# Another order of GpSimd's round in the attention stage of a two-layer mixture-of-experts kernel

## The reference

```python
x = x + L0_ffn(L0_cond(x, W1, b1, v, itok_B_0_2), wg, w1, w2, w3, sw1, sw2, sw3)
x = x + L1_ffn(L1_cond(x, itok_B_0_30, W, b), ln1.., Wqkv, Wproj, ln2.., Wgate, W1, b1, W2, b2)
```

```python
# end of layer 0: each token adds up the rows that its 4 experts left for it, weighed
y = zeros.at[buf_tok].add(out * buf_w)
# layer 1, per sequence b
h = layernorm(xc); q, k, v = h @ Wqkv; q, k = rope(q), rope(k)
x = xc + (softmax(mask(q @ k.T / 4)) @ v) @ Wproj        # residual
h2 = layernorm(x); gates = softmax(h2 @ Wgate); top_inds = top_k(gates, 2)
exp_in = zeros((E, capacity, d)).at[e_flat, p_eff].set(flat[t_flat])   # table of tokens
```

## Time and profile before

| What | Value |
|---|---|
| median of 3 runs | 1586.76 us |
| profiled execution | 1577.03 us, its span 1575.2 us |
| mean granted TensorE clock | 0.955 |
| gathers `got` L1421 | 128, 127.3 us busy on POOL |
| power `rs` L1402 | 32, median 725 ns |
| residual sum L1398 on POOL | 14, median 1285 ns |
| table entries L1440 | 64, median 996 ns |

### The profile page before, as it was taken

One profiled execution on the slowest core, in us unless ns is written; L12 is line 12 of the kernel. 1 busy time (PEld: TensorE's weight loads), 2 busy tenths in 40 slices (PEclk: granted clock), 3 DMA queues, 4 the chain that ended last, 5 costly groups with the idle time before them and its releaser, 6 DMA issues.

```text
span 1575.2 us, 27518 instructions
## 1 busy us (share of the span) xinstructions
PE 1413.4 (90%) x9777; PEld 1227.6 (78%) x9777; DVE 1037.4 (66%) x2455; ACT 911.7 (58%) x2160; POOL 716.4 (45%) x710
## 2 busy tenths in 40 slices
PE   7987699999999998689999989889838999999996
PEld 5876589999999997557767767667727999999996
DVE  2999367766767775667877878767634565565552
ACT  5886245545455553157877777777914564465452
POOL 0788533333433304444555655554253454454443
PEclk9998899999999999889999999999958999999998
DMA  5421346565666623545755645663433342343212
GB/s 169 145 68 36 87 139 162 162 167 169 171 171 170 174 71 119 103 85 99 144 108 122 149 92 114 112 138 66 88 119 91 93 109 54 67 104 87 47 22 27
DMA packets 134648, 174.13 MB, mean 111 GB/s; under 512 B 21525, under 2 KB 106336, under 8 KB 134512
## 3 DMA queue, kind: packets, MB, share of 16 engines
q1 hardware_dynamic: 105872, 119.63, 28.9%
q0 software_dynamic: 28160, 51.96, 16.6%
q10 hardware_dynamic: 480, 0.79, 0.3%
HBM read 107.28 MB, written 42.08 MB: 95 GB/s over the span
## 4 chain that ended last, share of the span: by engine, by line
PE 67%; DVE 12%; issue 7%; another core or an unknown queue 6%; ACT 5%; POOL 2%; SPq 1%; DMA 1%; DVEq 0%; POOLq 0%; ACTq 0%
PE banks L942 41%; PE banks L1491 4%; PE banks L1448 4%; PE banks L1544 3%; PE banks L451 2%; PE banks L1004 2%; ACT PN L1597 2%; DVE hidden L977 2%; PE banks L1504 2%; PE banks L1465 1%; DVE lo_w L911 1%; PE banks L1506 1%; DVE lane_at L517 1%; DVE X L1713 1%
## 5 line engine op out<-in xcount | busy, mean ns | idle before, releaser
L942 PE MATMUL banks<-hi_x,hi_w 128*128 128x320 f32 (+1 forms) x832 | 293.9, 353 | 33.3 <-DVE hidden L977 26.1
L942 PE MATMUL banks<-lo_x,hi_w 128*128 128x320 f32 (+1 forms) x832 | 288.7, 347 | 0.0
L942 PE MATMUL banks<-hi_x,lo_w 128*128 128x320 f32 (+1 forms) x832 | 288.1, 346 | 0.0
L942 PE MATMUL banks<-hi_w,hi_h 128*128 128x256 f32 x896 | 260.4, 291 | 2.4 <-DVE X L1031 2.0
L884 POOL DMA_INDIRECT xe<-pooled,idx x160 | 154.7, 967 | 230.5 <-PE banks L1004 185.5
L942 PE MATMUL banks<-lo_w,hi_h 128*128 128x256 f32 x896 | 253.4, 283 | 0.0
L942 PE MATMUL banks<-hi_w,lo_h 128*128 128x256 f32 x896 | 253.4, 283 | 0.0
L942 PEld LDWEIGHTS banks<-hi_x,hi_w 128*128 128x128 f32 x832 | 160.5, 193 | 55.7 <-DVE hidden L977 29.9
L1904 POOL DMA_INDIRECT out<-X,tab x64 | 106.2, 1660 | 200.6 <-DVE X L2007 186.0
L1421 POOL DMA_INDIRECT got<-done,slot x128 | 127.3, 995 | 138.9 <-DMA done<-res 57.4
L1597 ACT ACTIVATE PN<-banks,smax 128x256 f32<-128x256 f32 (+1 forms) x512 | 180.0, 442 | 12.8 <-DVE smax L1703 12.8
(11 more groups left out here) (187 smaller groups left out, 3055.4 us busy)
## 6 DMA issues: line engine op xcount, KB each, us to landing
w<-in_L_ffn_w SPq DMA_DIRECT2D x96, 256.0 KB
done<-res SPq DMA_DIRECT2D x32, 640.0 KB
BIG<-in_L_ffn_W SPq DMA_DIRECT2D x16, 1024.0 KB
QS<-parts_qk SPq DMA_DIRECT2D x100, 128.0 KB
KS<-parts_qk SPq DMA_DIRECT2D x90, 128.0 KB
mask<-in_c_masks SPq DMA_DIRECT2D x16, 257.0 KB, 2.9
pooled<-XF SPq DMA_DIRECT2D x16, 256.0 KB, 3.2
WS<-in_L_cond_W SPq DMA_DIRECT2D x16, 256.0 KB
```

The lines of the kernel that those rows point to most:

```text
L942: last = e.matmul(o, a[i], b[j], start=start and k == 0, stop=stop and k == 2, skip_group_check=True)
```

## The change

The order of GpSimd's round is another, and so are seven of the eight numbers that hold its gathers back. No instruction is added or taken out. The instruction streams of TensorE, VectorE, ScalarE and SP are word for word the same.

```diff
     POOL_ROUND = (
-        ("entry", -3, 0), ("entry", -3, 1), ("qk", 1, 0), ("qk", 1, 1), ("entry", -3, 2), ("entry", -3, 3),
-        ("got", 3, 0, 0), ("got", 3, 0, 1), ("got", 3, 0, 2), ("got", 3, 0, 3), ("base", -2), ("got", 3, 1, 0),
-        ("norm", -1, 1), ("got", 3, 1, 1), ("norm", 2, 0), ("got", 3, 1, 2), ("got", 3, 1, 3))
+        ("qk", 1, 0), ("qk", 1, 1), ("got", 3, 0, 0), ("got", 3, 0, 1), ("got", 3, 0, 2), ("entry", -3, 0), ("base", -2),
+        ("got", 3, 0, 3), ("got", 3, 1, 0), ("norm", -1, 1), ("got", 3, 1, 1), ("norm", 2, 0), ("entry", -3, 1),
+        ("got", 3, 1, 2), ("entry", -3, 2), ("got", 3, 1, 3), ("entry", -3, 3))
...
-    GOT_PACE = (3, 4, 5, 6, 7, 7, 7, 9)
+    GOT_PACE = (0, 3, 4, 6, 7, 7, 9, 10)
```

## The result

| | before | after |
|---|---|---|
| median of 3 runs | 1586.76 us | 1569.3 us (1568.36 to 1572.67) |
| ratio | | 0.9902, 95% interval 0.9879 to 0.9925 |
| profiled execution, span | 1577.03, 1575.2 us | 1568.36, 1566.6 us |

The forecast was 1585.8 us and the range 1579 to 1594. The kernel is 17.5 us faster, more than the range and more than the first rival (1580) allowed.

The account below looks back on a forecast made before the run. It took TensorE, ScalarE and VectorE as a ring bounding the attention stage, POOL following. Only the first two gathers gained, 1 us, other terms 0: 1586.76 to 1585.8 us; own range 1583 to 1589, 8 in 10 range 1579 to 1594.

Parts of the forecast that it names:

- first rival: Faster: in 5 rounds the residual sum held VectorE's comparison and ScalarE's x1T; moving it gives 7 us, 1580 us; chance 0.19.
- The ring: The attention stage as a ring of TensorE, ScalarE and VectorE, with POOL (GpSimd) following it.
- Residual sum: GpSimd's sum beside VectorE's routing comparison, moved ahead of the fourth gather: cost 0, 7 us either side in 5 rounds.
- First two gathers: The first starts 3.3 us earlier in a round, VectorE's wait for tile 0 shrinks: 0 to 1.6 us, taken as 1.
- Fourth gather: Behind the moved entry and sum, it starts 0 to 2.6 us later, still in time for its combine: cost 0.
- Last two gathers: Eighth waits for reduction 10, starts 2.3 us later, takes 4 to 4.5; 6.85 us left before tile 1's combine: cost 0.
- second rival: Slower: the eighth gather becomes the bound at combine of tile 1, +8 us, 1594 us, at worst +35; chance 0.16.
- Rotary sums: GpSimd's sums after the round's last gather and an entry, which end 2.8 us before them: cover remains, cost 0.
- Powers: GpSimd's two powers that VectorE needs, behind the same gathers at the same pace of 7: cost 0.
- End of the stage: Three entries move behind the power before the last, near 1131.52; idle time shrinks from 4.62 to 0.5 us: cost 0.
- The signs named for "I am wrong": For the residual sum: x1T moves with it and the rounds get shorter by over 1 us.
- The sign for the last gather: VectorE waits for gathers in most rounds.

Follow-up runs that it names:

- chip A: The chip of follow-up runs where no profile has a wait on "remote" in this stage nor late time; the kernel before takes 1496 to 1498 us.

## Why the prediction was wrong

**What bounds the kernel.** The ring was read rightly, but of waits without a name I followed only the one of the earlier trace rows. The view of waits has two rows of them at these copies, 31.4 us in 14 waits; the late time is 37.7 us in 12 rounds, 3.1 us a round. None of this had a place in the sum.

**Residual sum: the step that failed.** "I cost it at 0, between -1.4 us and +1.4 us a round, 7 us in 5 rounds to either side." The place of the sum was worth some 14 us, on a chip with pauses: 0.9914 with it alone. The first rival had the right edit and named the right instruction (x1T), but it priced the gain by the comparison, which stands in 5 rounds and is worth 0 (chip A). In the kernel after, x1T's own waits, one of which the earlier trace rows showed, are what went: 16.8 us in 7 waits, some 12.5 us over the 0.6 us that each x1T waits on chip A too. I had noted that such a wait stands in rounds without the comparison too, and took that as speaking against the rival. It was the reason to count all rounds. The rival's cause was wrong all the same: with the sum last in the round x1T keeps its waits and the gain is there. How the place of the sum acts on TensorE's lag stays open.

**Pace: left out as well.** The prediction has the pace in its first and last gathers, at 1 us and at 0. Alone it was worth some 11 us where TensorE pauses (0.9928), and cost 0.3% on chip A. The entries, taken at 0 too, cost 1.2% alone. So 0.9902 is what is left of parts that are each larger than the few us given to them.

**First two gathers: place right, gain wrong.** The first starts at 964.99, 0.17 us behind the rotary sums. The two waits for tile 0 of before (1.6 us) are gone, but three others came (2.2 us); with those of tile 1 VectorE waited 5.1 us for gathered rows, against "under 3".

**Fourth gather: right.** Issued at 947.49, its combine began at 956.80 without a wait for it.

**Last two gathers: the duration right, the room wrong.** The eighth took 963.93 - 959.72 = 4.2 us; 4 to 4.5 was taken. The room was to be 6.85 us and was 963.24 - 959.72 = 3.5, since, as I read it, a round that loses a pause ahead of its combine loses the cover too. On the chip of the first result VectorE waited twice for tile 1, 2.9 us of the 5.1; on chip A seven times, 10.4 us of 13.8 in 11 waits, and there the 12 rounds took 327.9 us against 325.0. The second rival is real, small, and was outweighed.

**Rotary sums: cost right, cover wrong.** POOL was to wait over 2 us for the products of tile 0. In the round shown it doesn't wait at all: the entry ends at 962.01 and the sums start there. TensorE's waits for the sums are one of 3.3 us before and after.

**Powers: right.** VectorE's waits for them are 0.5 us in all, none over 0.3.

**End of the stage: cost right.** Seven entries in a row end before the next slots are there, and the idle time behind them is 3.68 us, not the 0.5 expected: from the first of them to the entry behind that wait it is now 12.5 us, where it was 9.6. POOL after, the answer to the earlier trace rows:

```profile
1120.43 1.16 POOL L1440 DMA_INDIRECT table<-pair,slot  x1 [0.19 <-issue]
...
1132.97 0.98 POOL L1440 DMA_INDIRECT table<-pair,slot  x1 [3.68 <-DVE slot L320]
...
1146.44 1.09 POOL L1402 TENSOR_TENSOR rs<-ve,nhalf 128x2 f32<-128x2 f32 x1 [8.65 <-DVE ve L1664]
```

**The sum.** The signs named for "I am wrong" on the residual sum came true: x1T moved, and the rounds got shorter by 1.7 us each. The sign for the last gather did not: VectorE waited for gathered rows five times in the stage.

**What stays open.** What a pause of TensorE is, and why it gets shorter or fails to come when VectorE and GpSimd are shifted by a microsecond. No kernel here changed TensorE's own work, so this wasn't tried. The late time follows the length of the 12 rounds in most of the twelve profiles with pauses (18.1 to 23.6 us in the four of the change, whose rounds take 335.8 to 342.7; 37.7 and 40.2 before, 356.9 and 356.2; 54.0 with the entries alone, 367.5), but not with the sum last in the round (39.1, 347.0). It is a sign that goes with the gain, not a shown cause.

Open too is the half clock near block 14: 6.8 or 10.2 us of it in each of the six profiles that have the entries' new places on chips with pauses, 3.4 us or none there in the others. From block 14 to 15 those six take 26.6 to 28.3 us, the other six with pauses 22.5 to 24.0, and all eight of chip A 22.5, with either place of the entries. So with pauses the entries' new places go with some 5 us lost at this one point.

## What to carry to other kernels

Before weighing edits add up the waits in which the semaphore comes well after the modelled end of the bounding engine's instruction, those with a name and those without: where they make some per cent of the stage, any edit that shifts the engines against each other can move the time by that much, in either direction, and the bounds of the range have to hold it in every round and not only where two events coincide. A gain from mere shifting can belong to the chip it was measured on, as 1% did here; measure it on a chip of the other kind before keeping it. When a stage gets shorter, the cover of each transfer behind it gets shorter too.

## What the runs showed of the hardware

Chips differ by 5 to 6% on the same program (1496 to 1498 us against 1575 to 1587), one core busy, with the same granted clock of 1.00 in the steady stages. The experts of layer 0, which no kernel changed, show it best. VectorE's multiplication behind TensorE in the kernel before, one expert and the next, first on the first chip and then on chip A:

```profile
409.59 0.49 DVE L977 TENSOR_TENSOR hidden<-gate,banks 128x320 f32<-128x320 f32 x1 [1.96 <-remote]
...
422.11 0.49 DVE L977 TENSOR_TENSOR hidden<-gate,banks 128x320 f32<-128x320 f32 x1 [1.92 <-remote]
```

```profile
408.07 0.49 DVE L977 TENSOR_TENSOR hidden<-gate,banks 128x320 f32<-128x320 f32 x1 [0.27 <-PE banks L942]
419.80 0.49 DVE L977 TENSOR_TENSOR hidden<-gate,banks 128x320 f32<-128x320 f32 x1 [0.27 <-PE banks L942]
```

An expert takes 12.52 us on the one and 11.73 on the other. The windows of 240 us there, in the same order:

```profile
300.00:540.00 240.00, 229.69 (x1692) 224.71 (x1690) 168.94 (x327) 122.86 (x268) 91.64 (x95) 1.00 0.60 166
```

```profile
300.00:540.00 240.00, 240.00 (x1799) 239.88 (x1798) 181.68 (x349) 130.04 (x289) 89.34 (x93) 1.00 0.62 175
```

At the same granted clock TensorE executes 1692 matmuls on the one and 1799 on the other, 6% more; on chip A it has no idle time at all. In these two rows the pause comes once in an expert of dense matmuls, about 1.9 us of wait where chip A has 0.27, of which 0.8 us reach the period. The granted clock doesn't show it; idle time ahead of VectorE and ScalarE behind a late semaphore does, without a name where it lags by over 1.5 us.
